# The fold of the down weights on POOL, and the sigmoid of b by ScalarE's tanh, in a delta-rule layer with an FFN

## The reference, cut to what matters

```
xn = layernorm(x)
# branch 1: gated delta rule, 32 heads of 64
qkvz = xn @ w_qkvz.T;  b, a = split(xn @ w_ba.T)
q, k, v = causal convolution over time, 4 taps, of q, k, v
g    = -exp(A_log) * softplus(a + dt_bias)          # decay of the state
beta = sigmoid(b)
q, k = l2norm(q) / 8, l2norm(k)
for t: S = S * exp(g_t); delta = (v_t - k_t S) * beta_t; S = S + k_t delta; o_t = q_t S
y1 = (rmsnorm(o) * norm_weight * sigmoid(z)) @ w_out.T
# branch 2: FFN between Walsh-Hadamard transforms
h  = fwht(xn * SU_ug);  h = silu(h @ W_gate.T * s1) * (h @ W_up.T * s2)
y2 = fwht(h * SU_dp) @ W_down.T * Wscale_dp          # fwht over 1024
out = x + y1 + y2
```

## Time and profile before

| what | us |
|---|---|
| timed runs | 885.0, 885.98, 876.76 |
| their median | 885.0 |
| the profiled execution, whole | 881.22 |
| the profiled execution, span from its first to its last instruction | 879.4 |
| TensorE matmuls, busy | 802.5 (91%) |
| VectorE, busy | 705.0 (80%) |
| ScalarE, busy | 324.9 (37%) |
| POOL, busy | 277.7 (32%) |

### The profile page before, as it was taken

One profiled execution on the slowest core, in us unless ns is written; L12 is line 12 of the kernel. 1 busy time (PEld: TensorE's weight loads), 2 busy tenths in 40 slices (PEclk: granted clock), 3 DMA queues, 4 the chain that ended last, 5 costly groups with the idle time before them and its releaser, 6 DMA issues.

```text
span 879.4 us, 29218 instructions
## 1 busy us (share of the span) xinstructions
PE 802.5 (91%) x12586; PEld 548.9 (62%) x12586; DVE 705.0 (80%) x1224; ACT 324.9 (37%) x737; POOL 277.7 (32%) x186
## 2 busy tenths in 40 slices
PE   1699999988999999999999999999998989989885
PEld 1345566666766666766766676666665766676664
DVE  4899988885888989797988889898979777976533
ACT  3245432432515334443435143434443343432110
POOL 3052305134161605133241615142534406070101
PEclk9999999999999999999999999999999999999898
DMA  8141411404031313213231314124051303110201
GB/s 239 34 95 18 129 24 21 102 19 99 11 70 39 79 39 64 67 23 64 58 70 34 79 39 91 40 45 91 13 103 23 81 10 69 26 32 15 37 3 48
DMA packets 129151, 49.34 MB, mean 56 GB/s; under 512 B 110976, under 2 KB 120576, under 8 KB 128896
## 3 DMA queue, kind: packets, MB, share of 16 engines
q1 hardware_dynamic: 128400, 47.34, 24.8%
q10 hardware_dynamic: 624, 0.15, 0.1%
HBM read 39.85 MB, written 7.60 MB: 54 GB/s over the span
## 4 chain that ended last, share of the span: by engine, by line
PE 66%; DVE 18%; DMA 4%; issue 4%; SPq 3%; ACT 2%; POOL 1%; POOLq 0%; DVEq 0%; ACTq 0%
PE bank L664 19%; DVE kq L250 6%; PE bank L727 5%; PE bank L685 5%; PE bank L845 5%; PE bank L815 3%; PE bank L785 3%; PE bank L755 3%; PE bank L769 3%; PE bank L796 3%; PE bank L750 3%; PE bank L692 2%; PE bank L759 2%; PE bank L757 2%; PE bank L818 2%
## 5 line engine op out<-in xcount | busy, mean ns | idle before, releaser
L664 PE MATMUL bank<-xnT,wq 128*128 128x512 f32 x512 | 251.0, 615 | 6.9 <-DVE kq L250 6.9
L250 DVE SCALAR_TENSOR_TENSOR kq<-bank,cw,kq 128x510 f32<-128x510 f32 (+2 forms) x288 | 214.5, 745 | 15.5 <-ACT kq L951 8.1
L1126 POOL TENSOR_TENSOR Sd<-St,dec 128x256 f32<-128x256 f32 x32 | 23.5, 734 | 370.3 <-DVE St L369 287.3
L664 PEld LDWEIGHTS bank<-xnT,wq 128*128 128x128 f32 x512 | 89.9, 192 | 80.4 <-issue 68.0
L1120 POOL TENSOR_TENSOR kqg<-kq,rows 128x1024 f32<-128x1024 f32 x32 | 77.3, 2422 | 112.0 <-issue 59.8
L951 ACT ACTIVATE kq<-bank,cw 128x512 f32<-128x512 f32 x96 | 65.8, 685 | 116.8 <-PE bank L664 52.5
L1130 POOL TENSOR_TENSOR ost<-ost,cst 128x8 f32<-128x8 f32 x32 | 53.5, 1673 | 65.8 <-DVE ost L381 64.9
L815 PE MATMUL bank<-d,ATP 64*64 64x64 f32 x1024 | 69.1, 234 | 3.5 <-ACT d L1013 1.9
L845 PE MATMUL bank<-wo,oT 128*128 128x256 f32 x256 | 70.8, 395 | 0.8 <-DVE oT L393 0.8
L727 PE MATMUL bank<-kq 64*64 64x128 f32 x1024 | 69.1, 274 | 0.9 <-DVE kq L250 0.5
L815 PEld LDWEIGHTS bank<-d,ATP 64*64 64x64 f32 x1024 | 57.1, 140 | 15.4 <-ACT d L1013 10.2
(11 more groups left out here) (132 smaller groups left out, 1314.2 us busy)
## 6 DMA issues: line engine op xcount, KB each, us to landing
rows<-decay_rows SPq DMA_DIRECT2D x64, 256.0 KB, 4.9
wq<-wqkvz_dram SPq DMA_DIRECT2D x16, 512.0 KB
inverse_blocks<-UU SPq DMA_DIRECT2D x16, 256.0 KB, 2.0
wguT<-wgu_dram SPq DMA_DIRECT2D x8, 256.0 KB, 3.3
woraw<-wout_dram SPq DMA_DIRECT2D x16, 128.0 KB, 2.6
base_blocks<-ATP SPq DMA_DIRECT2D x128, 16.0 KB, 1.8
UU<-base_blocks SPq DMA_DIRECT2D x16, 128.0 KB
U<-inverse_blocks SPq DMA_DIRECT2D x128, 16.0 KB, 2.0
```

What stands on the lines that cost most here:

```text
L250: nc.vector.scalar_tensor_tensor(out=y[:, :, t:S], in0=p[:, :, 0:S - t], scalar=cw[:, m, i // 2, 3 - t:4 - t], in1=y[:, :, t:S], op0=ALU.m ...
L664: last = nc.tensor.matmul(ring[i % 2][:], wq[:, q, kc, i // 2, :], xnT[:, kc, (i % 2) * 512:(i % 2) * 512 + 512], start=kc == 0, stop=kc = ...
```

## The change

1. VectorE loses `wscaled` (L441, two instructions), the two single butterflies and the step `0.fold` (L437, six instructions). POOL gets these eight instructions, with the same operands, behind its power L1139 and ahead of its order. Each waits for the one before it, through a new semaphore `fold_step`. TensorE's `wd` and POOL's `kqg` of pair 0 now wait for `fold_step` 8.
2. ScalarE's L1049 computes tanh(b / 2) instead of exp(-b). VectorE's L509 and L510 are replaced by one `tensor_scalar`, beta = -0.5 * tanh(b / 2) - 0.5, which stands behind L498 and ahead of the wait for the transposed decays.

```diff
# VectorE
-                def fold(m, q):
-                    for t in range(2):
-                        butterfly(wds[0], wds[1], 2, t)
-                    for t in range(2):
-                        butterfly(wds[1], wds[0], 4, t)
-                    steps["fold"] = count[0]
...
-                dve.wait_ge(wdn_in, 16)
-                dve.wait_ge(wsd_in, 16)
-                wscaled(0)
-                wscaled(1)
                 dve.wait_ge(rstd_done, 1)
...
                 dve.wait_ge(const_in, 16)
-                butterfly(wds[1], wds[0], 1, 0)
                 for q in (1, 3):
...
-                butterfly(wds[1], wds[0], 1, 1)
                 dve.wait_ge(ba_ready, 1)
...
                 steps["g"] = count[0]
 
+                step(nc.vector.tensor_scalar(beta[:], ga[:, 4, :, :], -0.5, -0.5, ALU.mult, ALU.add))
                 dve.wait_ge(rows_ready, 1)
...
                 dve.sem_inc(rows_made, 1)
-                step(nc.vector.tensor_scalar(ga[:, 0, :, :], ga[:, 4, :, :], -1.0, -1.0, ALU.mult, ALU.add))
-                step(nc.vector.reciprocal(beta[:], ga[:, 0, :, :]))
...
-0.proj.0 0.proj.1 0.fold 0.proj.2 0.proj.3
+0.proj.0 0.proj.1 0.proj.2 0.proj.3
# TensorE, wd
-                    pe.wait_ge(v_step, steps["fold"])
+                    pe.wait_ge(fold_step, 8)
# ScalarE
-                nc.scalar.activation(ga[:, 4, :, :], ga[:, 0, :, :], ACT.Exp, scale=-1.0).then_inc(a_step, 1)
+                nc.scalar.activation(ga[:, 4, :, :], ga[:, 0, :, :], ACT.Tanh, scale=0.5).then_inc(a_step, 1)
# POOL
                         if m == 0:
-                            pool.wait_ge(v_step, steps["fold"])
+                            pool.wait_ge(fold_step, 8)
...
                 nc.gpsimd.tensor_tensor(st[:, 3, :], st[:, 0, :], k("neghalf")[:, 0:TT], ALU.pow).then_inc(rstd_done, 1)
+                def fold(ins, n):
+                    ins.then_inc(fold_step, 1)
+                    pool.wait_ge(fold_step, n)
+
+                pool.wait_ge(wdn_in, 16)
+                pool.wait_ge(wsd_in, 16)
+                for i in range(2):
+                    fold(nc.gpsimd.tensor_tensor(wds[1][:, 4 * i:4 * i + 4], wds[0][:, 4 * i:4 * i + 4], wsd[:].unsqueeze(1).broadcast_to([P, 4, HID]), ALU.mult), i + 1)
+                for level, (src, dst) in enumerate(((wds[1], wds[0]), (wds[0], wds[1]), (wds[1], wds[0]))):
+                    s4, d4 = (w.rearrange("p (a t h) d -> p a t h d", t=2, h=1 << level) for w in (src, dst))
+                    for t in range(2):
+                        fold(nc.gpsimd.tensor_tensor(d4[:, :, t], s4[:, :, 0], s4[:, :, 1], (ALU.add, ALU.subtract)[t]), 3 + 2 * level + t)
```

More of the change, by code:

```diff
@@ L159, in layer @@
                    sq_done rstd_done xnT_ready xnT_used ba_ready a_step rows_ready e0_zero rows_made rows_out hug_made
-                   xh_ready xh_done wd_ready wd_used cwv_done fo_ready fo_acc""".split()
+                   xh_ready xh_done wd_ready wd_used fold_step cwv_done fo_ready fo_acc""".split()
         (w_in, row_in, wo_in, nw_in, ff_in, at_out, nb_in, uu_out, ui_in, proj_done, tap0_done, conv_step, z_done,
@@ L167, in layer @@
          mean_done, sq_done, rstd_done, xnT_ready, xnT_used, ba_ready, a_step, rows_ready, e0_zero, rows_made,
-         rows_out, hug_made, xh_ready, xh_done, wd_ready, wd_used, cwv_done, fo_ready, fo_acc) = (sem(x) for x in names)
+         rows_out, hug_made, xh_ready, xh_done, wd_ready, wd_used, fold_step, cwv_done, fo_ready, fo_acc) = (sem(x) for x in names)
         ring = [bank[0], bank[1]]
@@ L433, in _ @@
                     dve.sem_inc(mean_done, 1)
[L434 to L441, removed]
                 dve.wait_ge(sq_done, TT)
@@ L508, in _ @@
                 dve.sem_inc(rows_made, 1)
-                step(nc.vector.tensor_scalar(ga[:, 0, :, :], ga[:, 4, :, :], -1.0, -1.0, ALU.mult, ALU.add))
-                step(nc.vector.reciprocal(beta[:], ga[:, 0, :, :]))
                 program({"proj": proj, "ff": ff, "e": e, "stats": stats, "gram": gram, "vtr": vtr, "inv": inv, "hz": hz, "ks": ks,
-                         "state": state, "norm": norm, "gated": gated, "turn": turn, "out": out, "fold": fold, "fo": fo}, """0.proj.0 0.proj.1 0.fold 0.proj.2 0.proj.3 0.e 0.stats 0.proj.4 0.gram.0 0.proj.5 0.ff 0.gram.1 1.e 0.vtr.0 0.gram.2
-                         0.vtr.1 0.gram.3 1.proj.0 0.fo.0 1.proj.1 1.proj.2 0.fo.1 1.proj.3 1.stats 1.proj.4 1.gram.0 1.ff 1.proj.5 1.gram.1
-                         0.inv.0 0.inv.1 1.gram.2 0.inv.2 1.fo.0 1.gram.3 2.ff 2.e 1.fo.1 2.proj.0 2.proj.1 3.ff 2.fo.0 2.proj.2 2.proj.3 2.fo.1
+                         "state": state, "norm": norm, "gated": gated, "turn": turn, "out": out, "fo": fo}, """0.proj.0 0.proj.1 0.proj.2 0.proj.3 0.e 0.stats 0.proj.4 0.gram.0 0.proj.5 0.ff 0.gram.1 1.e 0.vtr.0 0.gram.2 0.vtr.1
+                         0.gram.3 1.proj.0 0.fo.0 1.proj.1 1.proj.2 0.fo.1 1.proj.3 1.stats 1.proj.4 1.gram.0 1.ff 1.proj.5 1.gram.1 0.inv.0
+                         0.inv.1 1.gram.2 0.inv.2 1.fo.0 1.gram.3 2.ff 2.e 1.fo.1 2.proj.0 2.proj.1 3.ff 2.fo.0 2.proj.2 2.proj.3 2.fo.1
                          0.hz.1.0 0.hz.1.1 1.vtr.0 0.hz.2.0 0.hz.2.1 3.fo.0 3.fo.1 0.hz.3.0 0.hz.3.1 1.inv.0 1.inv.1 0.state.0 1.vtr.1 0.ks.1
```

## The result

| | before | changed |
|---|---|---|
| median of the timed runs, same comparison | 885.49 us (876.76 to 889.22) | 899.91 us (897.43 to 902.02) |
| ratio, 95% interval | | 1.020 (1.0154 to 1.0245) |
| profiled execution, its span | 881.22, 879.4 us | 902.02, 899.9 us |

The kernel is slower, by 2.0% in this comparison; two later ones of the same changed kernel gave 1.0154 (1.011 to 1.0197) and 1.0132 (1.0086 to 1.0179). The forecast was slower, 896 us, by `xs` and the folds taking turns. The direction and the turns came as forecast; 899.91 lies above the 892 to 898 that the forecast gave itself.

A forecast was written before the change was run, and what follows sets the result against it. The first 50 us were taken as bound by a chain of dependent instructions, the rest by TensorE. Profiled 881.2 + 13.7 (first taps +14.6, less 0.9) = 894.9, plus 1.4, gives 896 us; range 879 to 901.

The forecast's parts named there:

- `xs` and the folds taking turns: At the start, POOL's folds block VectorE's `xs`, one per fold, 2.49 us a round; chance 0.50.
- the price of TensorE's pause: After idling, TensorE runs at low clock: 0.7 us added in the b/a product, 0.9 taken off behind the first taps.
- the b/a product: TensorE's product behind the transposes, before the first taps: 0.7 us longer by low clock, bounds 0 to 1.9.
- the projection behind the first taps: Four TensorE matmuls from 43.90: a shorter gap before them gains 0.9 us, bounds 0 to 1.9.
- the copy of `xnT`: Copy behind `xs` and the transposes: starts at 37.08 instead of 21.08, +16.0 us.
- `beta`: Two VectorE instructions before the first taps go, gaining 2.11 us; the replacement, about 0.3, hides in a wait.
- POOL was to be first: Next fold asks 0.08 us after a fold's end, next `xs` at 0.18, so one `xs` passes per fold.
- `pow`: POOL's power in LayerNorm takes 1.64 us instead of 2.61 once L441 is gone: gain 0.97.
- rival 1: Two `xs` pass per fold: first taps at +8.5, end +7.6, total 890 us; chance 0.20.
- rival 2: `xs` isn't blocked, only two-input VectorE instructions (L479 to L485) are: +3.1, total 886 us; chance 0.12.
- rival 3: Folds fall into VectorE's waits and POOL alone waits: faster, 878.6 us with no VectorE wait; chance 0.10.
- My own test: Wrong if first taps start before 41.5, or the end's difference isn't that at the taps within 2 us.

The follow-up runs named there:

- a0: The changed kernel again, unaltered, in a second comparison with the kernel before: ratio 1.0154 (1.011 to 1.0197).
- a1: The changed kernel once more, unaltered, in a third comparison with the kernel before: ratio 1.0132 (1.0086 to 1.0179).
- e4: Changed kernel, each fold's wait for the one before it sent through SyncE's queue, for a longer gap between folds: ratio 1.0099 against the kernel before.
- e7: As e4, with four more hops in SyncE's queue between one fold and the next: ratio 1.0073 against the kernel before.
- e2: Kernel before with only the POOL part: eight fold instructions on POOL, beta still by exp and reciprocal. Ratio 1.0201.
- e1: Kernel before with only the tanh form of beta; scaling and butterflies stay on VectorE. Ratio 0.9956.
- e3: Changed kernel with POOL's folds held back until VectorE has done all eight `xs`: ratio 1.0131 against the kernel before.
- e5: Changed kernel with POOL's folds held back until VectorE has made the decay rows: ratio 1.0114 against the kernel before.
- e6: On e1, no POOL fold: VectorE does one scaling beside `pow`, one behind `xs`, and first-level butterflies while waiting for the b/a product. Ratio 0.9954 against the kernel before.
- d1: Kernel before with nine more 8-column powers on POOL ahead of LayerNorm's own, delaying the start without POOL folds: ratio 1.0127.

## Where the prediction went wrong, and what of it held

**The step that failed** is the price of TensorE's pause. The sum added 0.7 us for the b/a product behind it, with 1.9 as the most, and took 0.9 off for the projection behind the first taps. Measured: the product is 2.14 us longer here and 2.65 and 2.91 longer in a0 and a1, each over the upper bound, and of the 0.9 the projection gave 0.10 (3.78 to 3.68), nothing in a0 and a1. What the product has instead of "low clock after a pause" is a slow rate of 53 ns per matmul for most of its length with a granted clock of 1.00; why is open. The total of the terms came out close all the same, and that is luck: the copy of `xnT` was put 0.86 too late and `beta` 0.41 too low, which made up for most of the product.

**A reason that failed.** POOL was to be first because the next `xs` starts only 0.18 after a fold's end. It starts at 0.07, and the fold at 0.08 goes first nevertheless (see e4 and e7).

**What held.** `pow` 1.64 us; eight folds from 14.76 (14.95 forecast), with 0.08 between them (0.27 forecast), the last ending at 34.01 (34.7); eight `xs` of 2.34 and then 2.49, one per fold; `beta` in its cover at 0.29; one table load; ScalarE's `kq` ahead of the third taps. e2 puts the whole loss on the fold, and rival 1 appears when the gap on POOL is long enough. Rivals 2 and 3 fell at the first row: `xs` is blocked, and POOL gives way once per round, not for good. (Rival 1's mark of +8.5 was added up wrong: its terms, 7.6 + 2.5 - 2.11, give 8.0.)

**Terms, to the third taps** (before to changed, first profile):

| term | forecast | measured |
|---|---|---|
| copy of `xnT` behind `xs` | +16.0 (at 37.08) | +15.14 (at 36.22) |
| b/a product longer | +0.7 | +2.14 (3.94 to 6.08) |
| `beta` | -2.11 | -2.52 |
| first taps | +14.6 | +14.76 |
| projection behind them, and the rest up to the third taps | -0.9 | -0.33 |
| third taps | +13.7 | +14.43 |

- *`xs`*: a round ends 0.14 after a fold and not 0.27, so it is 2.42 us from fold to fold and not 2.49. I had let `xs` run its last 0.27 alone. The 2.49 that the rows show for one `xs` is no contradiction: each starts 0.08 before the one ahead of it has ended. Another 0.2 us of the +15.14 is chance: LayerNorm's statistics (L427, 12.82; L444 before, 13.03) were that much earlier in this execution.
- *The product*: I added 0.7, with 1.9 as the upper bound. The bound came from four long matmuls behind a pause; these 128 short ones are slower by up to 3.1 us, and the profile of before, with 3.94, was one of the lucky ones. Of the five that start as early, e1 and e3 have 5.73 and 7.06, e5 and e6 3.95 and 3.94. So part of the +2.14 is the luck of the one profile of before; how much the pause itself costs these few can't tell.
- *`beta`*: 0.41 more, an idle stretch that I had shown in its row and not counted.
- *The projection*: the gap fell from 6.64 to 4.12 us and the four matmuls still took 3.68 (3.31 to 3.78 in the ten runs with this gap), against the 0.9 that I took back. The lower end of the bounds, nearly nothing, was right.

**The total.** The forecast was 896 and 899.9 was measured. As a difference it was +13.7; the third taps have +14.43 and the medians +14.4, +12.8 and +14.5. So 0.7 of the miss comes from the terms. The other 2.9 is the level that they were added to: 882.6, the mean of the runs shown, where the median in this comparison was 885.5. The two later comparisons have 882.5 and 883.2 for the kernel before and 895.3 and 897.7 for the changed one, so the level was a fair one and this comparison ran high on both sides, as its clock says for the changed kernel.

**My own test failed in the first profile**: the difference at the end was to be that at the taps within 2 us, and was 5.7 more. a0 and a1 hold it (-1.1 and +1.3), the medians of the first comparison do too (+14.4), and the spans scatter round their marks with both signs. What was wrong was the 2 us for a single profile, not the passing on of the delay.

**The price of the 10 us of moved work.** VectorE had done all eight in 10.0 us, 5.0 of them under the projection for nothing and 2.5 beside `pow`. POOL needs 18.7, and takes 16 us from VectorE while it does. The other places (e3, e5) and rhythms (e4, e7) tried on POOL don't mend it. Nor was the 0.97 of the `pow` a sure gain: in e1 and d1, where L441 is still there but starts after the first power, that power took 1.64 and 1.65.

## What to carry to other kernels

Before elementwise work is moved to POOL, count the VectorE instructions with two SBUF inputs or at double rate that run in the same stretch: each one waits for a whole POOL instruction (8 columns, 0.16 us alone, took 2.32), while those that read PSUM went free here. "Idle on POOL" is no room by itself, and a slack of 0.22 us behind a 5 us block means that the block was hidden and that nothing is won by moving it. In a kernel with a long bound tail judge an edit at the start by a mark close to it: here the third taps agree with the medians within 3 us in ten of eleven runs (all but d1; e5 waits later and isn't counted), while the end of a single profile is 4 to 6 us off to either side.

## What the runs showed of the hardware that was not expected

- A write-only POOL instruction stops VectorE's double-rate one for its whole length (1.97 for 0.41 us).
- Whose turn it is changes between a gap of 0.11 and one of 0.38 us on POOL: one `xs` per fold, or two. By the starts in the trace the blocked `xs` is the earlier one by 0.01 to 0.04 us.
- 128 small matmuls ran at two rates, 29 and 53 ns apart, with a granted clock of 1.00 at both, and the moment of the change differs from one execution to the next (3.94 to 7.06 us for the same product). Why is open.
- A pause of 4.12 us before the projection costs TensorE nearly as much as one of 6.64 (3.31 to 3.78 for 1.88 us of work).
